# Tile 0 of a ternary feed-forward and attention kernel: W_down's sum behind the third gate, constant products in TensorE's waits, the second tile's rows centred by GpSimd

## The reference

```python
x = x + 0.5 * ffn(layernorm(x))
x = x + attention(layernorm(x))     # 16 heads of 128, 4 key/value heads, rotary, causal
x = x + 0.5 * ffn(layernorm(x))     # the same weights as the first

def ternary_quant(w):
    scale = mean(abs(w)) + 1e-8
    return clip(round(w / scale), -1, 1) * scale

def ffn(x):                          # W_up, W_gate: 1024 x 256, W_down: 256 x 1024
    up, gate = x @ ternary_quant(W_up).T, x @ ternary_quant(W_gate).T
    return (silu(up) * gate) @ ternary_quant(W_down).T
```

## Time and profile before

| | us |
|---|---|
| median of three runs | 1089.22 |
| lowest and highest of them | 1087.47, 1089.34 |
| the profiled execution | 1088.83 |
| its span on the core | 1087.0 |
| PE, DVE, ACT, POOL busy in the span | 1069.8, 923.1, 815.8, 715.1 |

### The profile page before, as it was taken

One profiled execution on the slowest core, in us unless ns is written; L12 is line 12 of the kernel. 1 busy time (PEld: TensorE's weight loads), 2 busy tenths in 40 slices (PEclk: granted clock), 3 DMA queues, 4 the chain that ended last, 5 costly groups with the idle time before them and its releaser, 6 DMA issues.

```text
span 1087.0 us, 26892 instructions
## 1 busy us (share of the span) xinstructions
PE 1069.8 (98%) x8517; PEld 844.5 (78%) x8517; DVE 923.1 (85%) x2313; ACT 815.8 (75%) x2038; POOL 715.1 (66%) x906
## 2 busy tenths in 40 slices
PE   8999999999999999999999999999999999999998
PEld 5556566788888888888888888888888887566665
DVE  6787886899999999999999999999999997433333
ACT  6787997787888788887877878778787785444443
POOL 2566675777777777777777777777777774444443
PEclk9999999999999999999999999999999999999999
DMA  9522332234434343344333443334334343100101
GB/s 348 155 49 40 58 59 40 45 74 93 70 74 82 71 83 68 72 82 79 76 68 72 82 82 72 76 72 83 74 72 82 72 82 69 30 19 19 39 19 39
DMA packets 262166, 79.93 MB, mean 74 GB/s; under 512 B 249328, under 2 KB 260848, under 8 KB 261872
## 3 DMA queue, kind: packets, MB, share of 16 engines
q1 hardware_dynamic: 261696, 79.19, 35.1%
q10 hardware_dynamic: 432, 0.27, 0.1%
HBM read 12.85 MB, written 4.19 MB: 16 GB/s over the span
## 4 chain that ended last, share of the span: by engine, by line
PE 74%; issue 10%; POOL 6%; ACT 5%; DVE 4%; DMA 0%; POOLq 0%; DVEq 0%; ACTq 0%
PE bank L759 45%; PE bank L818 14%; POOL SCR L428 6%; PE bank L718 5%; PE bank L728 5%; PE bank L748 4%; ACT SCR L628 1%; DVE ARENA L1144 1%; ACT ARENA L635 1%; PE bank L677 1%; DVE SCR L962 1%; DVE bank L1168 1%; ACT SCR L502 0%; DVE X L952 0%; ACT SCR L517 0%
## 5 line engine op out<-in xcount | busy, mean ns | idle before, releaser
L453 POOL TENSOR_SCALAR SCR<-SCR,RI 128x128 f32<-128x128 f32 (+1 forms) x512 | 311.1, 608 | 44.2 <-DVE RI L1140 4.1
L628 ACT ACTIVATE SCR<-bank,NM 128x128 f32<-128x128 f32 (+1 forms) x512 | 208.5, 419 | 122.8 <-DVE NM L1168 122.7
L418 POOL TENSOR_TENSOR SCR<-SCR 128x512 f32<-128x512 f32 x160 | 203.4, 1271 | 146.0 <-DVE SCR L962 144.6
L428 POOL TENSOR_TENSOR SCR<-SCR 128x512 f16<-128x512 f32 x128 | 151.4, 1185 | 154.1 <-ACT SCR L517 152.0
L818 PE MATMUL bank<-SCR 128*128 128x128 f32 (+1 forms) x1024 | 193.7, 332 | 4.4 <-ACT SCR L628 3.3
L523 ACT COPY SCR<-bank 64x512 f32<-64x512 f32 x320 | 185.6, 580 | 14.2 <-PE bank L759 8.1
L981 DVE SCALAR_TENSOR_TENSOR SCR<-SCR,CS,bank 128x512 f32<-128x512 f32 x128 | 95.1, 743 | 115.9 <-PE bank L728 103.5
L1144 DVE TENSOR_TENSOR ARENA<-SCR,ARENA 128x768 f16<-128x768 f32 x128 | 186.7, 1459 | 4.8 <-ACT ARENA L635 3.9
L759 PE MATMUL bank<-WOH,ARENA 128*128 128x256 f16 x1024 | 188.3, 273 | 0.8 <-DVE X L1177 0.8
L1168 DVE CUSTOM_DVE_ANT_0 bank<-bank,MASK,SCQ 128x128 f32<-128x128 f32 (+1 forms) x512 | 182.8, 415 | 3.5 <-PE bank L818 2.7
L534 ACT ACTIVATE SCR<-bank,SU 128x512 f32<-128x512 f32 x128 | 87.7, 685 | 110.7 <-PE bank L718 110.5
(11 more groups left out here) (120 smaller groups left out, 1649.1 us busy)
## 6 DMA issues: line engine op xcount, KB each, us to landing
out<-X SPq DMA_DIRECT2D x7, 512.0 KB, 2.9
X<-in_x SPq DMA_DIRECT2D x1, 2560.0 KB, 11.2
ARENA<-in_wq SPq DMA_DIRECT2D x1, 2048.0 KB, 13.9
ARENA<-in_wo SPq DMA_DIRECT2D x1, 2048.0 KB, 18.8
SCR<-ARENA SPq DMA_TRANSPOSE x128, 3.6
X<-in_x SPq DMA_DIRECT2D x3, 512.0 KB, 9.9
X<-in_wu SPq DMA_DIRECT2D x2, 512.0 KB, 5.6
X<-in_wg SPq DMA_DIRECT2D x2, 512.0 KB, 7.4
```

Of the source, the lines that this page charges most:

```text
L418: gp.tensor_tensor(dst, M1[:, m, :], M2[:, m, :], ALU.add).then_inc(add, 1)
L428: gp.tensor_tensor(HL[layer][:, f % 4, :], H32[layer][:, f % 2, :], HH[layer][:, f % 4, :], ALU.subtract).then_inc(s["hl_done"], 1)
L453: last = gp.tensor_scalar(EX[:, par, lo:hi], EX[:, par, lo:hi], RI[:, par, c:c + 1], PS, ALU.mult, ALU.mult)
L628: last = act.activation(EX[:, par, 384 * hh + lo:384 * hh + hi], SBK[hh][:, lo:hi], ACT.Exp, bias=NM[:, par, c:c + 1], scale=-1.0, accum_o ...
```

## The change

It edits the work of tile 0 of the first layer only.

- W_down's magnitudes are summed in two passes of 1024 columns (`down_sizes`), one behind the signs of piece 0, one behind the high part in piece 1. total(2) adds both and stands behind gate(2), not gate(0). The scales of W_down are made in piece 2.
- Signs stand behind the high part of their piece, and are dealt out anew by SIGNS; so are the ternary pieces by TERNARY. W_down's first quarter and (0, 2) go from piece 1 to piece 2, (2, 1) of the signs from 2 to 3, (1, 3) of the ternary pieces from 4 to 3, the sign of (2, 2) from 4 to 5 and of (2, 3) from 5 to 6.
- `keep_warm`: two products ahead of total(1), five between up(0) and gate(0), six instead of four ahead of up(0).
- The sums for the norm of the second tile stand in piece 1 of VectorE, its `rstd` behind hl(1) of GpSimd, and GpSimd centres the rows itself with four TENSOR_SCALAR instructions (`second_center`), where ScalarE did with four ACTIVATE instructions in piece 2. The high part stays in piece 3 of ScalarE.

```diff
-        TERNARY = {-1: [(0, 0), (1, 0)], 0: [(0, 1), (1, 1)], 1: [(2, 0), (0, 2)], 2: [(1, 2)], 3: [(2, 1), (0, 3)], 4: [(1, 3)],
-                   5: [(2, 2)], 7: [(2, 3)]}
+        TERNARY = {0: [(0, 1), (1, 1)], 2: [(2, 0), (0, 2), (1, 2)], 3: [(2, 1), (0, 3), (1, 3)], 5: [(2, 2)], 7: [(2, 3)]}
-        SIGNS = {0: [(0, 1), (1, 1)], 1: [(2, 0), (0, 2)], 2: [(1, 2), (2, 1)], 3: [(0, 3), (1, 3)], 4: [(2, 2)], 5: [(2, 3)]}
+        SIGNS = {0: [(0, 1), (1, 1)], 2: [(2, 0), (0, 2), (1, 2)], 3: [(2, 1), (0, 3), (1, 3)], 5: [(2, 2)], 6: [(2, 3)]}
-        norm_job(1, 1, -1, 2, 3, 3)
+        norm_job(1, 1, 1, 3, 3, 3)
@@ GpSimd, rstd
                 gp.tensor_tensor(RSTD[:, :], VE[:, :], NEGHALF[:, :], ALU.pow).then_inc(ln_rs, 1)
+                if isinstance(q, int) and q == 1:
+                    second_center()
+            def second_center():
+                gp.wait_ge(ln_t0, DC)
+                gp.wait_ge(ln_rs, 2)
+                for s in range(SUB):
+                    gp.tensor_scalar(XN[:, s // 2, :, s % 2, :], X[:, (SUB + s) * D:(SUB + s + 1) * D].rearrange("p (c d) -> p c d", c=DC),
+                                     MV[:, s, 0:1], RSTD[:, s:s + 1], ALU.subtract, ALU.mult).then_inc(ln_xn, 1)
+                gp.wait_ge(ln_xn, 2 * SUB)
@@ GpSimd
             rstd(0)
-            rstd(1)
@@ ScalarE
+            def down_sizes(c):
+                act.wait_ge(ffn_raw[2], 16)
+                cols = slice(c * E, (c + 1) * E)
+                act.activation(MAGNITUDES[2][:, cols], RD[:, cols], ACT.Abs, accum_out=PSUMS[:, 4 + c:5 + c]).then_inc(f_part[2], 1)
@@ ScalarE, piece
-                if layer == 0 and n == 0:
-                    for i, q in SIGNS.get(f, ()):
...
                 if layer == 0 and n + f == 0:
-                    act.wait_ge(ffn_raw[2], 16)
-                    act.activation(MAGNITUDES[2], RD, ACT.Abs, accum_out=PSUMS[:, 4:5]).then_inc(f_part[2], 1)
+                    signs(f)
+                    down_sizes(0)
                 if f > 0:
                     high(layer, n, f - 1)
                 elif not isinstance(n, int) or n > 0:
                     high(layer, n - 1, FC - 1)
+                if layer == 0 and (n, f) == (0, 1):
+                    down_sizes(1)
+                if layer == 0 and n == 0 and f > 0:
+                    signs(f)
                 if layer == 0:
                     for q, tile in norms("center", n, f):
-                        norm_center(q, tile)
+                        if q != 1:
+                            norm_center(q, tile)
@@ TensorE, total
-                halves = (2, 2, 1)[i]
-                pe.wait_ge(f_part[i], halves)
+                pe.wait_ge(f_part[i], 2)
@@ TensorE, up
                         if a == 1:
+                            keep_warm(2)
                             total(1)
...
                 last.then_inc(s["u_done"], 1)
+                if making and f == 0:
+                    keep_warm(5)
@@ TensorE, ffn
-                    if layer == 0 and isinstance(n, int) and n + f == 0:
+                    if layer == 0 and (n, f) == (0, 2):
                         total(2)
@@ TensorE
             first_turn()
-            keep_warm(4)
+            keep_warm(6)
@@ VectorE
+                        if q == 1:
+                            ve.wait_ge(xin[1], 16)
+                            ve.wait_ge(ln_rs, 1)
...
-                    if f == 1:
+                    if f == 2:
                         ternary_scale(2)
...
             ternary(-1)
-            ve.wait_ge(xin[1], 16)
-            ve.wait_ge(ln_rs, 1)
-            stats(1, 1)
```

More of the change, by code:

```diff
@@ L125, in program @@
         HS = sb("HS", [P, HEADS], F32)
-        PSUMS = sb("PSUMS", [P, 5], F32)
+        PSUMS = sb("PSUMS", [P, 6], F32)
         FSC = sb("FSC", [P, 4], F32)
@@ L496, in norm_center @@
                 act.wait_ge(ln_nb, q)
[L497 to L500, removed]
+                act.wait_ge(ln_lo, q - 1)
                 for s in range(SUB):
@@ L517, in high, with signs @@
                 act.copy(HH[layer][:, f % 4, :], H32[layer][:, f % 2, :]).then_inc(s["hh_done"], 1)
+            def signs(f):
+                for i, q in SIGNS.get(f, ()):
+                    act.wait_ge((ffn_raw2[0], ffn_raw2[1], ffn_raw[2])[i], 16)
+                    raw, t = quarter(i, q)
+                    act.activation(t, raw, ACT.Sign).then_inc(signed, 1)
+            def down_sizes(c):
+                act.wait_ge(ffn_raw[2], 16)
+                cols = slice(c * E, (c + 1) * E)
+                act.activation(MAGNITUDES[2][:, cols], RD[:, cols], ACT.Abs, accum_out=PSUMS[:, 4 + c:5 + c]).then_inc(f_part[2], 1)
             def rope_swap(r, m, src):
@@ L534, in piece @@
                 act.activation(SG[layer][:, f % 2, :], UB[f % 2][:, :], ACT.Silu, scale=SU16[:, 0:1]).then_inc(s["silu_done"], 1)
-                if layer == 0 and n == 0:
-                    for i, q in SIGNS.get(f, ()):
-                        act.wait_ge((ffn_raw2[0], ffn_raw2[1], ffn_raw[2])[i], 16)
-                        raw, t = quarter(i, q)
-                        act.activation(t, raw, ACT.Sign).then_inc(signed, 1)
                 if layer == 0 and n + f == 0:
-                    act.wait_ge(ffn_raw[2], 16)
-                    act.activation(MAGNITUDES[2], RD, ACT.Abs, accum_out=PSUMS[:, 4:5]).then_inc(f_part[2], 1)
+                    signs(f)
+                    down_sizes(0)
                 if f > 0:
@@ L684, in total @@
                     pe.wait_ge(f_sc, 1)
-                halves = (2, 2, 1)[i]
-                pe.wait_ge(f_part[i], halves)
-                for c in range(halves):
-                    last = pe.matmul(FTOT[i], ONES[:, :], PSUMS[:, 2 * i + c:2 * i + c + 1], start=c == 0, stop=c == halves - 1)
+                pe.wait_ge(f_part[i], 2)
+                for c in range(2):
+                    last = pe.matmul(FTOT[i], ONES[:, :], PSUMS[:, 2 * i + c:2 * i + c + 1], start=c == 0, stop=c == 1)
                 last.then_inc(f_tot, 1)
```

## The result

| | us |
|---|---|
| changed kernel, median of 20 runs (lowest to highest) | 1090.96 (1089.33 to 1092.46) |
| kernel before, median of 20 runs beside them | 1088.87 (1087.47 to 1090.0) |
| ratio, with its 95% interval | 1.002 (1.0014 to 1.0026) |
| profiled execution of the changed kernel, and its span | 1089.78, 1088.0 |

The change makes the kernel 2.1 us slower, where 3.1 us faster was forecast. Its first transposes also start 0.18 us later than in the trace of before, because x landed that much later (VectorE's first sums start at 4.71 instead of 4.53 us); where starts are compared, such a difference is taken off.

What follows compares the result with a forecast made beforehand. TensorE was taken to bound the kernel; 3.1 us of waits and 1.1 of clock, less 0.3 for constant products, 0.4 behind GpSimd and remaining new waits, gave -3.15 us: 1086.1 us, range 1084.6 to 1088.9.

Steps and rivals of the forecast that it cites:

- centring on GpSimd: Second tile's norm: ScalarE loses four instructions of 2.07 us, GpSimd gets four at 0.50 us; down(2) starts 0.38 us late.
- GpSimd's centring is dear, and the kernel gets slower: Rival: hl(2) and down(2) queue behind four dear steps; gain nil at 1.32 us; chance 0.08 for 1.0-1.8 us, 0.05 for more.
- The price of a step, 0.50 us: Each GpSimd centring step taken at 0.50 us from line 453's median 0.48, bounded by 0.37 and 2.01 us.
- The exclusion of VectorE and GpSimd: Two-SBUF-operand VectorE instructions and GpSimd's exclude each other: 1.16 us of waits in centring, ending 25.90 us; costs up(8) 0.38 us.
- The sum from there: From centring's end at 25.90 us, down(2) at 28.19 and up(8) at 34.26 us against 37.41: -3.15 us.
- The constant products: Tile 0's added products delay total(1) by 0.27 to 0.3 us, cost gate(0) nothing; leaving two and five out gains 0.25 us.
- W_down's sum behind the third gate: TensorE's 1.94 us wait ahead of total(2) goes; a 0.89 us wait ahead of down(0) takes its place.
- Last signs and pieces: Ternary piece (1,3) is there at 27.1 us against gate(6) at 29.9, so gate(6)'s 0.86 us wait goes.
- The transpose: Second tile's transpose lands at 33.7 us, 0.55 us ahead of up(8); costs nothing until landing takes over 5.0 us.
- The clock: TensorE stays at 2.4 GHz behind the shorter waits of 0.2 to 0.9 us; 1.14 of 1.5 us arrive at up(8).
- The first rival: The clock falls anyway in another place, perhaps ahead of down(0): time 1088.3 to 1089.1 us, chance 0.12.
- It is given back later: Rival: behind tile 0, a fixed-time transfer or VectorE in the middle stretch takes the lead: 1089.2 us, chance 0.07.

Runs made afterwards that it cites:

- the run of the forms: Changed kernel plus sixteen GpSimd instructions at its end, two of each form: centring 1.22 us, two multiplications by two per-row scalars 0.556, by one 0.472.
- the run of multiply and add: Changed kernel with GpSimd's centring as multiply and add instead of subtract and multiply: 1087.52 us against 1089.53 for the kernel before, ratio 0.9986.

## Why the prediction was wrong

The direction was wrong, and it failed at one step: *centring on GpSimd*, put at 0.50 us a step and measured at 1.22 us alone and 1.72 us on average in place. The rival "GpSimd's centring is dear, and the kernel gets slower" is what happened, with hl(2) and down(2) queued behind it as drawn there. It put the end of the gain at 1.32 us a step and gave 0.08 to steps of 1.0 to 1.8 us, 0.05 to dearer ones. By its two prices around 1.22 us (a gain of 1.25 us at 1.0, none at 1.32) the price alone would have left a gain of 0.4 us (an estimate); the 0.8 us of waits that were not in it make that 0.4 us of loss, which is what the trace shows at up(8), 37.81 against 37.37 us. Most of the rest of the 2.1 us is the clock behind the new wait.

- **The price of a step, 0.50 us.** It is 1.22 us by itself (the run of the forms): 2.9 us too little for four. The row chosen had the right shape and engine, but another operation. The bound from above, 2.01 us, was no price at all: it is an instruction of 128 columns, held out by two of VectorE's (shown beside the run of multiply and add). Of the reasons for and against that I named (two scalars, strided output) neither is the cause.
- **The exclusion of VectorE and GpSimd.** 1.16 us of waits for GpSimd were forecast, with VectorE waiting in its turn, so that the piece (1,3) was to be there at 27.1 us. GpSimd waits 2.0 us (6.86 less four times 1.22), VectorE nothing, and (1,3) is there at 26.5 us. The rows that I had showed VectorE waiting for a GpSimd instruction that had begun first. The same trace had the other order too: the low part of 28.70 us takes 1.50 instead of 1.16 us, where a ternary piece had begun at 28.43. The two centring steps that were held both began inside a run of VectorE's pieces and ended 0.9 us behind its last one, so that they also waited for pieces that began later than they did. The Trainium skill ("SBUF — State Buffer", section "SBUF: two separate sides") has the pair of ports go to whoever starts first. The traces agree as to which of two engines waits when one instruction of each meets; that VectorE's next pieces, each begun 0.08 us before the one ahead of it ends, keep GpSimd out as well is what the traces of the changed kernel, of multiply and add, and of line 453 show beyond it.
- **The sum from there.** Centring ends at 29.80 us (start taken off) instead of 25.90: 0.2 from a later start, 2.9 from the price, 0.8 from the waits. down(2) at 31.65 instead of 28.19 us, 3.46 late, and up(8) at 37.81 instead of 34.26, 3.55 late. The other starts that the prediction names, up to down(0), held to 0.2 us. The terms that the sum lists (3.1 + 1.1 - 0.3 - 0.4) leave 0.35 us for new waits, where its own text has 0.9 us ahead of down(0) and 0.3 us ahead of up(2); the schedule gave the 3.15 us, not this list, and with ScalarE's centring the schedule held.
- **The constant products.** Right: total(1) starts 0.3 us later, gate(0) waits for nothing, the price is 0.2 us (the trace without them). Whether the clock would hold without them I left open, and the runs without them do not settle it: two of nine have the lower mean clock, against one of nine.
- **W_down's sum behind the third gate.** Right, with the wait of 0.88 us ahead of down(0) in its place.
- **Last signs and pieces.** Right: no wait at gate(6) but 0.1 us.
- **The transpose.** Right: with ScalarE's centring it is issued at 29.1 us, takes 4.8 to land and is there 0.4 us ahead of up(8), where the forecast had 0.55. In the changed kernel it comes late with the centring (32.9 us, and 4.5 to land) and is there 0.6 us ahead.
- **The clock.** The old fall goes, but I did not see that a dear centring makes a wait twice as long as the old one, behind which the clock falls anew, by the mean clock in 16 of 20 runs. So the changed kernel's median has 1.2 us more than its profile. The first rival named a fall in another place, for instance ahead of down(0).
- **It is given back later.** No: from up(8) to the end of the span the traces of all versions, but the one with instructions added at its end, take 1049.4 to 1050.1 us.

With ScalarE's centring the same forecast (3.15 us less than before, 1086.1 us) would have been right to 0.3 us.

## What to carry to other kernels

A price is a price of an operation on an engine, not of a shape: when a step moves to another engine, the nearest row has to share the operation, and where it does not, an instruction of that form at the end of the kernel gives it in one run. The longest instruction of a row is worth a look at what ran beside it: here it showed that GpSimd can be kept out for a whole run of VectorE's instructions. When work moves to an engine that feeds the bound engine, ask what is queued behind it there; here one low part of 1.16 us waited behind 6.86 us of work that nobody needed so soon. And a wait that grows costs twice when the clock falls in it.

## What the runs showed of the hardware

- GpSimd's TENSOR_SCALAR on 128x256 float32 took 0.47 us for two multiplications with one per-row scalar, 0.556 with two, 0.55 for multiply and add, but 0.93 us for a subtraction alone and 1.14 to 1.22 for a subtraction with a multiplication.
- A GpSimd TENSOR_SCALAR that began inside a run of VectorE instructions with two SBUF operands each was held until the run ended (2.20 us instead of 0.55; 2.63 instead of 1.22; 2.01 instead of 0.37) and did not lengthen them. Two that began outside such a run kept their price (0.55 and 1.21 us), and beside the second of them VectorE's next piece took 0.87 us instead of 0.74.
- A GpSimd TENSOR_TENSOR that had begun first lengthened VectorE's piece (1.03 us instead of 0.74), and one that began during a piece was itself lengthened (1.50 instead of 1.16). Both forms thus fit the same reading, that the order of the starts decides; no long TENSOR_TENSOR began inside a run, so whether it would be held through one is not shown.
- Behind a wait of 3.66 us the granted clock fell to 0.50 in one traced execution of the changed kernel and not in the other; the mean clock puts 16 of 20 runs with the first. With the wait filled by constant products, none of 11 runs is under 0.999.
